# A recurrent pass with two-step triangular solves, products read straight from PSUM, and another order of steps on four engines

## The chip, the cores and the metric

The kernel runs on one core of one Trainium2 chip. The metric is the device time of one launch in microseconds (us): 3440.19 us, the median of three runs (3438.79 to 3451.68). TensorE multiplies matrices into PSUM (8 banks of 128 x 512 numbers), VectorE and ScalarE read PSUM and SBUF, GpSimd reads SBUF and issues the gathers, SyncE issues the other transfers. Each engine works through its own list in order and waits on semaphores where the code says `wait_ge`.

## What is computed

A layer norm, then two branches whose sum is added to the input. The attention branch is a gated delta rule over 16 sequences' halves of 128 tokens, for 16 key heads and 32 value heads of 128 columns; the other branch picks, for each token and each of 8 heads, 8 of 2048 experts, and mixes their rows.

```
mixed = silu(causal conv of width 4 over [q, k, v]);  q, k: l2norm
step: state = state * exp(g_t);  delta = (v_t - state·k_t) * beta_t
      state = state + k_t ⊗ delta;  o_t = state·q_t
y = rmsnorm(o * silu(z)) * norm_w;  attention = y @ w_out
z_e = silu((h · down_embed[e]) * softmax(score));  ffn = sum_e z_e * up_embed[e]
out = x + attention + ffn
```

The recurrence is done in chunks of 128 tokens. For each chunk the kernel solves a unit lower triangular system of 128 x 128, whose off-diagonal part is k·kᵀ times decay and beta.

## The kernel before

After a routing stage, which picks the experts and ends near 290 us, the kernel works through 64 passes (`PASSES`), written out one after another. A pass is one key head of one group of four token tiles; with two value heads (`R`) it has eight tasks, `task(b, c, r)`: b is one of two sequences, c the first or second chunk of it, r the value head. Passes are pipelined in two stages. The front of pass n+1 (projections, convolution, products, the inverses of the 16 x 16 diagonal blocks) is interleaved with the back of pass n (the rest of the inverse, the recurrence over c = 0 and 1, the output). Buffers with a 2 in their name alternate.

**Front.** TensorE: `differences` sums gates (ScalarE makes the decays `DT` with Exp), `projection(u)` for u = 0 (key), 1 (query), 2, 3 (values), 4, 5 (z). ScalarE takes a projection into `raw` and `qkv` (`take`), VectorE adds three `tap`s, ScalarE does `silu` and squares. `products(0)` is k·kᵀ; VectorE's `strict_part` masks it into `km`, and `triangle` makes the eight matrices `AT`. SyncE writes `AT` to DRAM and reads the diagonal blocks back to `bk`; VectorE inverts all of them at once (`eliminate`, `lower_products`, `lower_sums`, `lower_scaled`, `lower_block`, then a copy to `xrT`, `elim_v`); SyncE writes them out and reads them back as `X16` and `XT16` (`inv_in`). `products(1)` is k·qᵀ; `causal_part` masks it into `kq`, and GpSimd multiplies it by `DT` into `MT`.

**Back.** The inverse grows from blocks of 16 to 128 in three levels. Level `lv` is `level_E` on TensorE, a masking multiplication by VectorE (`level`, L1165), and `level_X`, which multiplies on the left and, except in the last level, also makes the other orientation; ScalarE takes both back (`take_X`, `take_XT`). Then for c = 0: `y0_t` = inverse · right side, VectorE scales it (`scaled_y`, L1287), the state `S` and the output; the same for c = 1 after VectorE has corrected the right side `RV` (L1362). `gated` makes `xg`, ScalarE sums its squares, VectorE makes `rms`, GpSimd's `finish` raises it to the power -0.5 and scales the eight tiles of `xg`, TensorE transposes them (`finish_transposes`, L491) and multiplies by `wo` (`finish_out`), VectorE adds to `acc` (`add_outputs`).

**Experts.** In each pass GpSimd gathers 16 rows (L952), in two runs of 8: the first after VectorE's level 1, the second after `mix_v`, the end of the mixing. Between them stands `finish`. VectorE does 16 `expert_dot`s at the pass's start and 16 steps of `expert_mix`.

GpSimd ends its pass with the power for the norms (`norm_p`, L980) and the two multiplications for `MT` (`mt_p`, L984). VectorE waits for `norm_p` after the dots. In VectorE's list `gated(0)`, which waits for `o0_t` from TensorE, stands between `lower_sums` and `lower_scaled`:

```
                if back:
                    dve.wait_ge(sm["yt_t"], at("yt_t", 2))
                    dve.wait_ge(sm["o0_t"], at("o0_t", 1))
                    gated(0, ps[:, 4, :], rq_b, z_b)
                if front:
                    lower_scaled()
```

## Time and profile before

| | us |
|---|---|
| median of three runs | 3440.19 |
| the profiled execution | 3440.67 |
| its span, first to last instruction | 3438.8 |
| TensorE busy | 2992.4 (87%) |
| VectorE busy | 3012.3 (88%) |
| ScalarE busy | 1794.2 (52%) |
| GpSimd busy | 2306.0 (67%) |

The span runs from the first to the last instruction of the program on the core; busy time counts an engine's own instructions, not its waits or its issuing of transfers. A busy share is a mean over routing, passes and tail, so what a step is worth is read in one pass. In a timeline each row is a run of like instructions: start, length, engine, line, what is written and read, how many, and in brackets how long the engine was idle before and what ended it.

### The profile page before, as it was taken

Reading aid. Unit: us, or ns where it says so; the run is one execution under the profiler, and the core shown is the slowest. Engines: PE = TensorE matmul, PEld = TensorE weight load, DVE = VectorE, ACT = ScalarE, POOL = GpSimd, SP = SyncE. Lnnn points to the kernel's source line nnn. Section 1 sums busy time; section 2 is a strip of 40 time slices with the busy share of each in tenths; the row PEclk is TensorE's granted clock in tenths of the full one; section 3 lists DMA queues with packets and bytes.
Section 4 is the critical chain, followed back from the end, with each engine's and each line's share of the span. In section 5 each row is a group of like instructions: output and inputs, shape, how many; then the busy total and the mean of one; then the engine's idle time right before and its main releaser. Section 6 shows DMA issues by size and latency. Waiting matters only on the chain.

```text
span 3438.8 us, 56504 instructions
## 1 busy us (share of the span) xinstructions
PE 2992.4 (87%) x18444; PEld 2451.1 (71%) x18444; DVE 3012.3 (88%) x9101; ACT 1794.2 (52%) x4111; POOL 2306.0 (67%) x2650
## 2 busy tenths in 40 slices
PE   7844999989998989899989988898989899998997
PEld 4422777778776777677767777777777777777776
DVE  5996999989998999899989898998899898989996
ACT  3322555555554555455545555555555555555553
POOL 0005777777767776777778777877777667877764
PEclk9976999999999999999999999999999999999999
DMA  1003545544555545454545554544555454544553
GB/s 60 1 1 104 137 132 141 135 131 132 137 139 135 131 133 139 130 133 133 141 126 138 134 138 124 149 127 134 138 138 137 125 139 132 146 129 135 144 132 89
DMA packets 541827, 427.98 MB, mean 124 GB/s; under 512 B 247008, under 2 KB 450784, under 8 KB 541536
## 3 DMA queue, kind: packets, MB, share of 16 engines
...
q14 instruction: 142, 1.16, 0.1%
...
## 4 chain that ended last, share of the span: by engine, by line
DVE 36%; POOL 35%; PE 14%; issue 9%; DMA 5%; ACT 1%; SPq 0%; DVEq 0%; POOLq 0%; ACTq 0%
POOL rows L952 22%; DVE rows L1193 9%; POOL xg L931 9%; DVE qkv L1177 6%; DVE mix L1210 4%; POOL rms L928 3%; DVE E L1165 3%; DMA rows<-table,pick 3%; PE ps L579 3%; PE ps L500 3%; PE ps L517 2%; PE ps L665 1%; DVE topi L1024 1%; DVE xg L1147 1%; PE ps L521 1%
## 5 line engine op out<-in xcount | busy, mean ns | idle before, releaser
L952 POOL DMA_INDIRECT rows<-table,pick x1024 | 1157.2, 1130 | 326.3 <-issue 326.3
L551 PE MATMUL ps<-X,AT 128*128 128x128 f32 x3072 | 417.7, 294 | 119.2 <-DMA XT<-whole 119.2
L551 PEld LDWEIGHTS ps<-X,AT 128*128 128x128 f32 x3072 | 392.9, 207 | 169.8 <-DMA XT<-whole 167.3
L806 ACT ACTIVATE qkv<-qkv 128x512 f32<-128x512 f32 x256 | 161.5, 631 | 518.6 <-DVE qkv L1177 518.6
L571 PE MATMUL ps<-XT,E 128*128 128x128 f32 x3072 | 400.6, 277 | 0.0
L801 ACT ACTIVATE raw<-ps 128x512 f32<-128x512 f32 x256 | 152.8, 597 | 433.2 <-PE ps L517 433.2
L1210 DVE SCALAR_TENSOR_TENSOR mix<-rows,zc,mix 128x256 f32<-128x256 f32 x896 | 375.1, 476 | 0.0
L571 PEld LDWEIGHTS ps<-XT,E 128*128 128x128 f32 x3072 | 368.9, 192 | 0.0
L939 POOL TENSOR_SCALAR gm<-cst,gn 128x128 f32<-128x128 f32 x512 | 362.9, 723 | 6.7
L1193 DVE CUSTOM_DVE_ANT_0 rows<-rows,h2c 128x128 f32<-128x128 f32 x1024 | 342.9, 399 | 9.2 <-SPq L328 4.7
L931 POOL TENSOR_SCALAR xg<-xg,rms 128x128 f32<-128x128 f32 x520 | 324.9, 637 | 7.0
L564 PEld LDWEIGHTS ps<-E,XT 128*128 128x128 f32 x2048 | 257.7, 193 | 98.1 <-DVE E L1165 56.5
L1177 DVE SCALAR_TENSOR_TENSOR qkv<-raw,cwv,qkv 128x510 f32<-128x510 f32 (+2 forms) x384 | 307.7, 802 | 6.8
L1177 DVE SCALAR_TENSOR_TENSOR qkv<-raw,cwkq,qkv 128x510 f32<-128x510 f32 (+2 forms) x384 | 285.7, 744 | 21.4 <-ACT qkv L802 12.1
L564 PE MATMUL ps<-E,XT 128*128 128x128 f32 x2048 | 274.1, 277 | 26.4 <-DVE E L1165 26.4
L943 POOL COPY pick<-idx_all 128x16 uint32<-128x16 uint32 x64 | 12.6, 196 | 421.9 <-DVE E L1165 421.9
L816 ACT ACTIVATE XT<-ps 128x512 f32<-128x512 f32 x384 | 228.0, 594 | 94.3 <-PE ps L571 86.4
L517 PE MATMUL ps<-xnT,Wkq 128*128 128x512 f32 x512 | 273.6, 661 | 0.0
L1165 DVE TENSOR_TENSOR E<-ps,cst 128x512 f32<-128x512 f32 x384 | 253.2, 682 | 14.6 <-PE ps L551 9.1
L517 PE MATMUL ps<-xnT,Wvz 128*128 128x512 f32 x512 | 254.2, 622 | 0.0
L500 PE MATMUL ps<-wo,yT 128*128 128x256 f32 x1040 | 247.6, 382 | 0.0
L521 PE MATMUL ps<-Wvz,xb 128*128 128x256 f32 x1024 | 243.1, 381 | 0.0
...
## 6 DMA issues: line engine op xcount, KB each, us to landing
...
whole<-AT SPq DMA_DIRECT2D x128, 256.0 KB, 3.6
X<-whole SPq DMA_DIRECT2D x128, 256.0 KB, 3.9
XT<-whole SPq DMA_DIRECT2D x128, 256.0 KB, 4.4
...
```

The costliest lines, as they stand in the source:

```text
L500: done = mm(ps[:, 2 + g, c * D:(c + 1) * D], yT[:, task(g, c, r), :], wo[:, r, :], start=r == 0, stop=r == R - 1)
L517: done = mm(ps[:, bank, :], w[:, k, :], xnT[:, k, bass.ds(pn * N, N)], start=k == 0, stop=k == KD - 1)
L551: done = mm(ps[:, g, (a % 4) * P:(a % 4 + 1) * P], AT_b[:, a, :], src[:, a, :], start=True, stop=True)
L564: done = mm(ps[:, 2 + g, (a % 4) * P:(a % 4 + 1) * P], src[:, a, :], E[:, a, :], start=True, stop=True)
L571: done = mm(ps[:, 4 + g, (a % 4) * P:(a % 4 + 1) * P], E[:, a, :], src[:, a, :], start=True, stop=True)
L931: pool.tensor_scalar(xg[:, a, :], xg[:, a, :], rms[:, a:a + 1], None, ALU.mult).then_inc(sm["y_p"], 1)
L939: pool.tensor_scalar(gm[:, a, :], mask(C_LE), gn[:, a:a + 1], None, ALU.mult).then_inc(sm["gm_p"], 1)
L952: pool.indirect_dma_start(rows[:, m, :], None, table[:, :], bass.IndirectOffsetOnAxis(ap=pick[:, m:m + 1], axis=0)).then_inc(gathered, 16)
L1165: V.tensor_tensor(E[:, 4 * g:4 * g + 4, :], ps[:, g, :].rearrange("p (a i) -> p a i", a=4), mask(C_MS + lv, 4), ALU.mult)\
L1177: ins = V.scalar_tensor_tensor(out=o, in0=i, scalar=w, in1=o, op0=ALU.mult, op1=ALU.add)
L1193: st.did(V.tensor_tensor_reduce(out=rows[:, k, 0:P], in0=rows[:, k, 0:P], in1=h2c[:, :], scale=1.0, scalar=0.0, op0=ALU.mult, op1=ALU.add, ...
L1210: sums[s] = st.did(V.scalar_tensor_tensor(out=mix[:, s, :], in0=rows[:, m, P:ROW], scalar=zc[:, 1, m:m + 1], in1=mix[:, s, :], op0=ALU.mul ...
```

## The change

- **Two steps, then halves.** The levels for 32 and 64 remain (`level_E`, `level_X` with lv 0 and 1), and `level_X` makes one orientation. In the first, VectorE copies the off-diagonal blocks into `E0`, whose diagonal is set once, with a predicated copy; then it turns the result with its own transpose (`turn_X`) for the other orientation. In the second, ScalarE copies two blocks of 32 x 32 per task into `E1` (`take_E`). The last level is gone. Each chunk's solve is now four steps: `blocks` (both halves' own inverses), `carried` (the lower half's correction from the upper 64 rows), `lower_rhs` on VectorE, `blocks` again.
- **Products from PSUM.** `km` and `kq` are gone. GpSimd makes the decays causal (`causal`, an affine select over 128 x 512), ScalarE multiplies them by beta and the key norm (`scale_decays`), and VectorE multiplies them with the products in PSUM: two instructions for `AT`, two for `MT`. Beta goes into the decays; the sign is in `AT`, and its diagonal is no longer set.
- **GpSimd.** `gm` is made by two affine selects, not eight multiplications; `finish` comes first, then both runs of gathers (the first waits for `half_v`, VectorE's mixing of the first four experts); the copies `pick` and `h2c` and the `MT` multiplications are gone.
- **VectorE.** The dots come in two runs of eight; the order is new, with `gated(0)` behind the elimination.
- `xb` and its transfer are gone; TensorE reads `xnT`.

```diff
-LEVELS = [16, 32, 64]
...
+    off = (p // (2 * BL) == j // (2 * BL)) & (p // BL == j // BL + 1)
...
-        E = sb("E", [P, TASKS, P])
-        Y = E
+        E0 = sb("E0", [P, TASKS, P])
+        E1 = sb("E1", [P, TASKS, P])
+        Y = sb("Y", [P, 2, 4, P])
...
-                def level_E(lv):
...
+                def level_E(lv, g):
...
                 def level_X(lv, g):
...
-                    if lv < len(LEVELS) - 1:
-                        for a in range(4 * g, 4 * g + 4):
-                            done = mm(ps[:, 2 + g, (a % 4) * P:(a % 4 + 1) * P], src[:, a, :], E[:, a, :], start=True, stop=True)
-                        done.then_inc(sm["x_t"], 1)
...
+                    E, src = (E1, XT) if lv else (E0, XT16)
                     for a in range(4 * g, 4 * g + 4):
                         done = mm(ps[:, 4 + g, (a % 4) * P:(a % 4 + 1) * P], E[:, a, :], src[:, a, :], start=True, stop=True)
                     done.then_inc(sm["xt_t"], 1)
...
+                def blocks(c, bank):
+                    return four(bank, c, lambda b, r, a: XT[:, a, :], lambda i, a: RV[:, a, :])
+
+                def carried(c, bank):
+                    return four(bank, c, lambda b, r, a: AT_b[0:64, a, :], lambda i, a: Y[0:64, c, i, :])
...
+                    pe.wait_ge(sm["exp_done"], at("exp_done", 2))
+                    products(0)
+                    pe.wait_ge(sm["tap_s"], at("tap_s", 2))
+                    squares(0, 7)
...
+                        pe.wait_ge(sm["e_v"], at("e_v", g + 1))
...
+                        level_X(0, g)
+                    for g in range(2):
+                        pe.wait_ge(sm["x_v"], at("x_v", g + 1))
+                        level_E(1, g)
...
+                        pe.wait_ge(sm["xt_s"], at("xt_s", g + 1))
+                        pe.wait_ge(sm["e_s"], at("e_s", 2 * g + 2))
+                        level_X(1, g)
...
+                    blocks(0, 1).then_inc(sm["y0_t"], 1)
...
+                    pe.wait_ge(sm["top0_s"], at("top0_s", 1))
+                    carried(0, 0).then_inc(sm["u0_t"], 1)
...
+                    pe.wait_ge(sm["at_v"], at("at_v", 2))
+                    products(1)
+                    squares(1, 5)
...
+                    pe.wait_ge(sm["u0_v"], at("u0_v", 1))
+                    blocks(0, 1).then_inc(sm["w0_t"], 1)
...
+                    pe.wait_ge(sm["ys0_s"], at("ys0_s", 1))
...
+                    blocks(1, 0).then_inc(sm["y1_t"], 1)
...
+                    pe.wait_ge(sm["top1_s"], at("top1_s", 1))
+                    carried(1, 1).then_inc(sm["u1_t"], 1)
+                    finish_out(0)
+                    pe.wait_ge(sm["u1_v"], at("u1_v", 1))
+                    blocks(1, 0).then_inc(sm["w1_t"], 1)
+                    finish_out(1)
+                    pe.wait_ge(sm["ys1_s"], at("ys1_s", 1))
+                    four(4, 1, lambda b, r, a: MT_b[:, a, :], lambda i, a: Y[:, 1, i, :]).then_inc(sm["o1_t"], 1)
...
+                def take_E(g):
+
+                    act.wait_ge(sm["e_t"], at("e_t", 3 + g))
+                    for p in (32, 96):
+                        A(E1[p:p + 32, 4 * g:4 * g + 4, p - 32:p], ps[p:p + 32, g, :].rearrange("p (a i) -> p a i", a=4)[:, :, p - 32:p],
+                          ACT.Copy).then_inc(sm["e_s"], 1)
...
+                    if lv == 0:
+                        act.wait_ge(sm["x_v"], at("x_v", g + 1))
...
+                def scale_decays(r):
+
+                    for a in range(r, TASKS, R):
+                        A(DT[:, a, :], DT[:, a, :], ACT.Copy, scale=scol[:, a:a + 1]).then_inc(sm["scaled_s"], 1)
+
+                def take_Y(c, rows, bank):
+                    return A(Y[0:rows, c, :, :], ps[0:rows, bank, :].rearrange("p (i d) -> p i d", i=4), ACT.Copy)
...
+                    act.wait_ge(sm["s_v"], at("s_v", 1))
+                    act.wait_ge(sm["causal_p"], at("causal_p", 2))
+                    scale_decays(0)
...
+                    scale_decays(1)
...
+            def causal(dst, src, done):
+
+                pool.affine_select(dst, src, [[0, 4], [1, P]], ALU.is_ge, zero, base=0, channel_multiplier=-1).then_inc(done, 1)
...
-                for a in range(TASKS):
-                    pool.tensor_scalar(gm[:, a, :], mask(C_LE), gn[:, a:a + 1], None, ALU.mult).then_inc(sm["gm_p"], 1)
...
+                for g in range(2):
+                    causal(gm[:, 4 * g:4 * g + 4, :], gn[:, 4 * g:4 * g + 4].unsqueeze(2).broadcast_to([P, 4, P]), sm["gm_p"])
...
+                for g in range(2):
+                    pool.wait_ge(sm["exp_done"], at("exp_done", g + 1))
+                    d = DT[:, 4 * g:4 * g + 4, :]
+                    causal(d, d, sm["causal_p"])
...
-                    pool.wait_ge(sm["e_v"], at("e_v", 3))
-                picks(f)
-                pool.tensor_copy(h2c[:, :], h2_all[:, bass.ds(f // 4, 1), :].rearrange("p a c -> p (a c)"))
-                gather(0)
+                    finish()
+                    pool.wait_ge(sm["half_v"], at("half_v", 1))
+                gather(f, 0)
                 if n is not None:
-                    finish()
                     pool.wait_ge(sm["mix_v"], at("mix_v", 1))
-                gather(K // 2)
+                gather(f, K // 2)
...
-                for g in range(2):
-                    pool.tensor_tensor(MT2[nx][:, 4 * g:4 * g + 4, :].rearrange("p (t r) i -> p t r i", r=R),
...
+                    V.copy_predicated(E0[:, 4 * g:4 * g + 4, :], mask(C_OFF, 4).bitcast(U32), ps[:, g, :].rearrange("p (a i) -> p a i", a=4))\
...
+                    V.transpose(X[:, 4 * g:4 * g + 4, :].rearrange("p a i -> p (a i)"), ps[:, 4 + g, :]).then_inc(sm["x_v"], 1)
...
-                    for a in range(4 * g, 4 * g + 4):
-                        st.did(V.scalar_tensor_tensor(out=AT[:, a, :], in0=km[:, a // R, :], scalar=scol[:, a:a + 1], in1=DT[:, a, :],
-                                                      op0=ALU.mult, op1=ALU.mult))
-                    st.wait()
-                    V.tensor_tensor(AT[:, 4 * g:4 * g + 4, :], AT[:, 4 * g:4 * g + 4, :], mask(C_ID, 4), ALU.add).then_inc(sm["at_v"], 1)
...
+                def triangle(r):
+
+                    dve.wait_ge(sm["scaled_s"], at("scaled_s", 4 * r + 4))
+                    V.scalar_tensor_tensor(out=of_head(AT, r), in0=keys_by_time(), scalar=-1.0, in1=of_head(DT, r), op0=ALU.mult, op1=ALU.mult)\
+                        .then_inc(sm["at_v"], 1)
...
+                def lower_rhs(c, bank, ready, done):
+
+                    dve.wait_ge(sm[ready], at(ready, 1))
+                    v = half_tasks(RV, c)[64:P].rearrange("p b r d -> p b (r d)")
+                    V.tensor_tensor(v, ps[64:P, bank, :].rearrange("p (b d) -> p b d", b=2), v, ALU.add).then_inc(sm[done], 1)
...
+                    for r in range(R):
+                        V.tensor_tensor(of_head(MT, r), keys_by_time(), of_head(DT, r), ALU.mult).then_inc(sm["mt_v"], 1)
...
                         dve.wait_ge(sm["norm_p"], last("norm_p"))
+                    second_outputs()
+                    second_gated(nx)
+                    dve.wait_ge(gathered[0], 128 * n + 128)
+                    expert_dots(0, (0, 1))
+                    expert_weights(0)
...
+                    key_norms()
+                if back:
+                    turn_X(0)
+                    turn_X(1)
...
+                    expert_mix(6, 8)
+
+                    st.wait()
+                    V.tensor_tensor(total, mix[:, 0, :], mix[:, 1, :], ALU.add).then_inc(sm["mix_v"], 1)
+                if front:
+                    lower_products()
+                    lower_sums()
+                    lower_scaled()
+                    lower_block()
+                    st.wait()
+                    V.tensor_copy(xrT[:, :, :], rows_of(xr).rearrange("n i c -> n c i")).then_inc(sm["elim_v"], 1)
+                if back:
+                    dve.wait_ge(sm["yt_t"], at("yt_t", 2))
+                    dve.wait_ge(sm["o0_t"], at("o0_t", 1))
+                    gated(0, ps[:, 4, :], rq_b, z_b)
+                    lower_rhs(1, 1, "u1_t", "u1_v")
+                if front:
+                    for u in (2, 3):
+                        for d in (1, 2, 3):
+                            tap(u, d)
```

On **TensorE**, before, from the last level's end to the second chunk's output (L571 level_X, L517 and L521 projections, L579 solves, state and outputs, L491 transposes, L500 output, L665 state products):

```order
L571 MATMUL ps<-XT,E 128x128 x8
L517 MATMUL ps<-xnT,Wvz 128x512 x2
L579 MATMUL ps<-RV,XT 128x128 x4
L491 MATMUL ps<-cst,xg 128x128 x8
L517 MATMUL ps<-xnT,Wvz 128x512 x2
L579 MATMUL ps<-E,Kd 128x128 x4
L579 MATMUL ps<-E,MT 128x128 x4
L500 MATMUL ps<-wo,yT 128x256 x4
L521 MATMUL ps<-Wvz,xb 128x256 x4
L665 MATMUL ps<-S,qkv 128x256 x4
```

Now, from the same place to the state products (L562 is every solve, L533 and L540 the products and squares of the front):

```order
L554 MATMUL ps<-XT,E 128x128 x8
L625 MATMUL ps<-cst,qkv 128x128 x2
L516 MATMUL ps<-xnT,Wvz 128x512 x2
L562 MATMUL ps<-RV,XT 128x128 x4
L490 MATMUL ps<-cst,xg 128x128 x8
L562 MATMUL ps<-Y,AT 128x128 x4
L533 MATMUL ps<-qkv 128x128 x4
L540 MATMUL ps<-ones,sq 128x1 x4
L562 MATMUL ps<-RV,XT 128x128 x4
L516 MATMUL ps<-xnT,Wvz 128x512 x2
L562 MATMUL ps<-Y,Kd 128x128 x4
L562 MATMUL ps<-Y,MT 128x128 x4
```

The solve of the first chunk has two groups more, and steps of the front stand between its steps.

On **VectorE**, before, the end of the elimination and of the pass:

```order
L1232 TENSOR_TENSOR prod<-bk,xr 64x512
L1240 TENSOR_REDUCE low<-prod 64x64
L1147 SCALAR_TENSOR_TENSOR xg<-ps,norm,z 128x256 x2
L1246 TENSOR_TENSOR prod<-xr,low 64x512
L1255 TENSOR_REDUCE xr<-prod 64x8x8
L1354 COPY xrT<-xr 64x256
```

Now, from the correction of `RV` (L1405) and the last mixing (L1260, L1410) on:

```order
L1405 SCALAR_TENSOR_TENSOR RV<-ps,neg,RV 128x128 x4
L1260 SCALAR_TENSOR_TENSOR mix<-rows,zc,mix 128x256 x4
L1410 TENSOR_TENSOR acc<-mix 128x256
L1285 TENSOR_TENSOR prod<-bk,xr 64x512
L1293 TENSOR_REDUCE low<-prod 64x64
L1299 TENSOR_TENSOR prod<-xr,low 64x512
L1308 TENSOR_REDUCE xr<-prod 64x8x8
L1417 COPY xrT<-xr 64x256
L1185 SCALAR_TENSOR_TENSOR xg<-ps,norm,z 128x256 x2
L1328 TENSOR_TENSOR RV<-ps,RV 64x2x256
```

`gated` (L1147, now L1185) has moved behind the elimination, and the mixing's end, which stood ahead of the elimination, into the middle of it.

On **GpSimd**, one pass before:

```order
L964 COPY cols<-gates 128x24
L966 COPY xr<-cst 64x256
L935 COPY gn<-gates 128x8
L939 TENSOR_SCALAR gm<-cst,gn 128x128 x8
L943 COPY pick<-idx_all 128x16
L973 COPY h2c<-h_all 128x128
L952 DMA rows<-table,pick 128x384 x8
L928 TENSOR_TENSOR rms<-rms,powers 128x8
L931 TENSOR_SCALAR xg<-xg,rms 128x128 x8
L952 DMA rows<-table,pick 128x384 x8
L980 TENSOR_TENSOR norm<-ss,powers 128x8
L984 TENSOR_TENSOR MT<-kq,DT 128x512 x2
```

and now:

```order
L1004 COPY cols<-gates 128x24
L1006 COPY xr<-cst 64x256
L977 AFFINE_SELECT DT<-DT 128x512 x2
L981 COPY gn<-gates 128x8
L977 AFFINE_SELECT gm<-gn 128x512 x2
L968 TENSOR_TENSOR rms<-rms,powers 128x8
L971 TENSOR_SCALAR xg<-xg,rms 128x128 x8
L992 DMA rows<-table,idx_all 128x384 x16
L1021 TENSOR_TENSOR norm<-ss,powers 128x8
```

The power and the scaling of `xg` stand ahead of all 16 gathers.

## Rows read from the trace of the kernel before

**Rows 1.** The page, part 1: busy time, share of the span, instructions of each engine.

```profile
PE 2992.4 (87%) x18444; PEld 2451.1 (71%) x18444; DVE 3012.3 (88%) x9101; ACT 1794.2 (52%) x4111; POOL 2306.0 (67%) x2650
```

**Rows 2.** Timeline of SyncE's queue: pass starts (L346), AT out (L353), last pass (L335).

```profile
1794.30 0.35 SPq L346 DMA_DIRECT2D Wvz<-wvz  x1
...
1809.47 2.23 SPq L353 DMA_DIRECT2D whole<-AT  x2
...
1841.89 0.34 SPq L346 DMA_DIRECT2D Wvz<-wvz  x1
...
3387.45 29.35 SPq L335 DMA_DIRECT2D wo<-woh  x2
```

**Rows 3.** Stretches: us, busy of PE, PEld, DVE, ACT, POOL; granted clock; DMA.

```profile
1794.30:1799.70 5.40, 5.37 (x21) 3.86 (x22) 5.30 (x27) 1.30 (x2) 4.56 (x7) 0.68 0.77 241
...
333.30:3388.20 3054.90, 2760.60 (x17517) 2308.23 (x17518) 2731.77 (x7591) 1682.59 (x3906) 2250.87 (x2574) 0.97 0.51 135
```

**Rows 4.** Timeline of TensorE, from one pass into the next.

```profile
1823.73 0.66 PE L491 MATMUL ps<-cst,xg 128*128 128x128 f32 x4 [1.66 <-POOL xg L931]
...
1841.92 2.70 PE L551 MATMUL ps<-X,AT 128*128 128x128 f32 x16 [1.88 <-DMA XT<-whole]
...
1850.77 1.95 PE L551 MATMUL ps<-X,AT 128*128 128x128 f32 x16
...
1857.12 1.06 PE L571 MATMUL ps<-XT,E 128*128 128x128 f32 x8
1858.01 1.06 PE L564 MATMUL ps<-E,XT 128*128 128x128 f32 x8
```

**Rows 5.** Timeline of VectorE, from one pass into the next.

```profile
1819.77 0.23 DVE L1222 TENSOR_TENSOR outer<-bk,xr 64x14 f32<-64x14 f32 x1 [0.55 <-DMA bk<-whole]
...
1821.89 0.74 DVE L1287 TENSOR_TENSOR E<-ps,scol 128x256 f32<-128x256 f32 x2
...
1828.00 0.88 DVE L1147 SCALAR_TENSOR_TENSOR xg<-ps,norm,z 128x256 f32<-128x256 f32 x2 [2.14 <-PE ps L579]
...
1830.61 0.37 DVE L1354 COPY xrT<-xr 64x256 f32<-64x256 f32 x1
...
1838.35 2.17 DVE L1193 CUSTOM_DVE_ANT_0 rows<-rows,h2c 128x128 f32<-128x128 f32 x1
...
1840.67 0.28 DVE L1193 CUSTOM_DVE_ANT_0 rows<-rows,h2c 128x128 f32<-128x128 f32 x1
...
1849.38 2.30 DVE L1177 SCALAR_TENSOR_TENSOR qkv<-raw,cwkq,qkv 128x510 f32<-128x510 f32 x3
...
1852.39 1.28 DVE L1165 TENSOR_TENSOR E<-ps,cst 128x512 f32<-128x512 f32 x2
...
1862.39 1.66 DVE L1210 SCALAR_TENSOR_TENSOR mix<-rows,zc,mix 128x256 f32<-128x256 f32 x4
```

**Rows 6.** Timeline of GpSimd, one pass, and one row of another pass.

```profile
1027.77 1.19 POOL L952 DMA_INDIRECT rows<-table,pick  x1 [5.07 <-issue]
...
1823.86 1.08 POOL L952 DMA_INDIRECT rows<-table,pick  x1 [0.18 <-issue]
...
1834.32 1.39 POOL L952 DMA_INDIRECT rows<-table,pick  x1 [0.30 <-issue]
1835.72 1.69 POOL L980 TENSOR_TENSOR norm<-ss,powers 128x8 f32<-128x8 f32 x1
1837.39 2.49 POOL L984 TENSOR_TENSOR MT<-kq,DT 128x512 f32<-128x512 f32 x2
...
1840.67 5.74 POOL L939 TENSOR_SCALAR gm<-cst,gn 128x128 f32<-128x128 f32 x8
...
1866.29 4.94 POOL L931 TENSOR_SCALAR xg<-xg,rms 128x128 f32<-128x128 f32 x8
```

**Rows 7.** Timeline of ScalarE, two rows of one pass.

```profile
1810.67 0.60 ACT L816 ACTIVATE XT<-ps 128x512 f32<-128x512 f32 x1
...
1816.24 1.16 ACT L870 ACTIVATE Kd<-ps,cols 128x128 f32<-128x128 f32 x4
```

422 lines of the change are left out of this document (186 added, 236 removed).

## The prediction

> **What bounds the kernel now.** I read the page first, then stretches, then the four timelines of one pass. The page has TensorE at 87% and VectorE at 88% [rows 1], so no engine is full, and the mean doesn't say what ends last. The passes start at SyncE's loads of `Wvz`, 1794.30 and 1841.89 [rows 2], 47.6 us apart, and all 63 full passes take 3054.9 us [rows 3], 48.5 each. So the question is which ring of waits closes in 47.6 us.
>
> Read backwards from TensorE's L551, which idles 1.88 us for the DMA of `XT` and starts at 1841.92 [rows 4]. That DMA hangs on VectorE's copy to `xrT`, ended at 1830.98 [rows 5]: 10.9 us out to DRAM and back. The copy stands behind `gated`, for which VectorE idled 2.14 us, waiting for TensorE's output of the first chunk [rows 5]. That sits behind TensorE's list from 1794.3 on, in which it waits once more, 1.66 us, for GpSimd's scaled `xg` [rows 4]. The ring is: TensorE's levels, the wait for GpSimd, the first chunk, `gated`, the elimination's end, two DMAs. Also, at the pass's start the granted clock is 0.68 over 5.4 us [rows 3], part of it at 1.2 GHz: 16 products take 2.70 us there and 1.95 later [rows 4]. It fell after TensorE had been idle for 1.88 us. A mean of 0.68 is 3.5 us at half speed, a loss of 1.7; the mean of 0.97 over all passes [rows 3] is 1.45 us lost in each.
>
> **What the change takes off that ring.** `gated` now stands behind the elimination, so the copy to `xrT` no longer waits for TensorE, and `level_E` waits behind `projection(0)`. TensorE loses two groups of four products in each of two `level_X`, one whole `level_E` and one whole `level_X`, eight groups; four are added by `carried` and the second `blocks`. A group is 0.89 us, start to start [rows 4]: 3.6 us less of TensorE's time. VectorE loses two pairs of masks (1.28 each, [rows 5]) for one pair of transposes, the `km` and `kq` products, and most of `triangle`; it gains two `MT` products and pays two `lower_rhs` for two `scaled_y`. It also loses 1.9 us at the first dot, which took 2.17 us against 0.28 for the others [rows 5], and ended 0.6 us after GpSimd's `MT` (1837.39 to 1839.88, [rows 6]). That multiplication has left GpSimd. `xb`, `pick` and `h2c` cost nothing on a ring: SyncE's queue and GpSimd both waited there.
>
> **The ring that takes its place.** Gathers 9 to 16 can't start before `mix_v`, since their rows are being read. GpSimd then does 8 gathers and the power, and VectorE's first instruction of the next pass, the addition to `QS`, now waits for `norm_p`. Before, the gathers started at 1823.86, 4.6 us after the mixing had ended, and VectorE needed the norms only behind 16 dots. I walk this ring once, from `norm_p` at 0:
>
> - `QS`, `gated`, eight dots with their weights, three taps: 0.7 + 0.9 + 2.15 + 2.2 = 5.95. (512 columns from PSUM 0.64, `gated` 0.88, dots 0.24 apart, taps 2.30 for three, [rows 5].) TensorE, freed 3.8 us before `norm_p`, has `projection(0)` done by then and `level_E` too, as `inv_in` comes 10.9 us after an elimination that ends 9.9 us before this point.
> - ScalarE's `silu` 0.7, then `products(0)`, `squares(0)` and two groups of `level_X`: 3.8, to 10.45.
> - The second transpose 0.65 (below), `take_XT` 0.6, eight scalings and two copies: 11.1, 11.85, then 4 x 0.29 + 0.6 + 4 x 0.29 to 14.9. (A copy 0.60, four scaled copies 1.16, [rows 7].) VectorE idles some 2.3 us here, filled only by one expert.
> - `AT` of the second head 0.7: 15.6. Two experts mixed 1.6 ([rows 5]: four steps 1.66), taps 2.4 with a short wait, eight dots 2.1: 21.7. `lower_rhs` 0.65 and `MT` 1.3 with 0.75 of waits for TensorE: 24.4. Two experts: 26.0.
> - The diagonal blocks are back by then: between the second half of `AT` going out (1809.47 to 1811.70, [rows 2]) and the first elimination step (1819.77, [rows 5]) lie 8.1 us, and 15.6 + 8.5 is 24.1. The whole elimination took 1830.98 - 1819.77 - 2.14 - 0.80 - 0.74 = 7.5 us [rows 5]; its first part, 3.6, stands on the ring: 29.6. `RV` 1.1, the last two experts and the sum 2.0: `mix_v` at 32.75.
> - GpSimd: from 1823.86 to 1835.72 eight gathers, 11.86, then the power 1.69, and 0.2 ahead [rows 6]: 13.75. `norm_p` at 46.5.
>
> The other end of the pass is shorter: after `mix_v` VectorE has 3.9 of elimination, `gated`, `lower_rhs`, six taps and the additions, 11.2 us, and TensorE's last product ends some 3.8 us before `norm_p`.
>
> **Prices that the trace doesn't show.** The predicated copy and the transpose: 128 x 512 out of PSUM in one instruction, so I take the mask's 0.64; half of that at best, double at worst. Doubled, the transposes add 1.3 on the ring and the copies 0.6. The Trainium skill's page Vector Engine (DVE) Microarchitecture Reference, section The reshape front-end and per-opcode configuration, states one element per cycle and lane for the transpose; no run here shows it. The affine selects: 1.25, as `MT`'s (two in 2.49) have the shape; from 0.4 to 2.9, the latter four times the 0.72 of a `gm` tile of a quarter the width (eight in 5.74, [rows 6]). GpSimd then reaches `finish` at 7.4, as VectorE's `rms` does, and ends it at 14.2 (1.7 + 0.1 + 5, [rows 6]), where TensorE wants it at 20; even at 2.9 it ends at 19.2. The first gathers wait for VectorE's fourth expert (17.2) and end at 28, before `mix_v`, so the selects are hidden up to 3.2 us each.
>
> **The clock.** TensorE idles 2.8 us ahead of `products(0)`, longer than the 1.88 after which it fell. If it falls, the 1.7 us are lost on the ring, since products, squares and `level_X` follow. Between 0 and 1.7 I take 1.0: 47.5 us a pass.
>
> **Stalls.** One gather in 113 begins after 5.07 us of idling [rows 6], seven times in the trace, always in the first run of eight; most of what lies between 47.6 and the mean of 48.5 us is theirs. Now the first run has 4.7 us to spare, so I take 1 us each, 7 in all.
>
> **Sum.** Routing and the first front 333.3 + 3 for two copies of `E0` and `E1`; 63 x 47.5 = 2992.5; the last pass and the tail as before, 3438.8 - 3387.45 = 51.4 [rows 2, 3]; 7 of stalls; 1.9 around the span: 3389 us. The profiled execution took 3440.67, the median is 3440.19, so they stand alike.
>
> **Rivals.** About 0.5%, 17 us, is what a measurement can tell from no change; that is 0.27 us a pass.
>
> - *A shorter ring.* The clock holds and the eight gathers, 9.8 to 10 us without company (eight of 0.95 and 0.30 between), end sooner, or the transposes cost half: 44.9 to 46.5 us, 3225 to 3326. For it: each select and copy that left GpSimd. Against: the eight gathers' 11.86 had VectorE's taps and elimination beside them, as they will now. From about 45 us on TensorE's last product sets the pass. Chance 0.22.
> - *One for one.* The `norm_p` ring and small waits I set at 0.1 make up what the DMA ring gave: 48.1 to 48.6 us, 3423 to 3457. Chance 0.12.
> - *Slower: VectorE held at the pass's start.* Four affine selects run at GpSimd from 0.5 to 6 us, just beside `gated`, the dots and the taps. If each holds VectorE as `MT` held the first dot, two pairs cost 1.9 each, all on the ring before `products(0)`: 51.3 at worst, 49.4 with one pair, 3509 to 3630. It decides from 1.1 us of holding on. The row of the first dot speaks for it; that the dots beside `gm` took 0.28 [rows 5, 6] speaks against. The Trainium skill's page GPSIMD Engine Reference, section Key points, names contention with VectorE's instructions that have two SBUF inputs, which a dot and a tap are; the trace agrees for `MT`, not for `gm`. Doubled prices of the new VectorE instructions, 49.4, fall in the same place. Chance 0.23.
> - *Slower: selects above 3.2 us each.* Then `finish` delays TensorE's transposes, and each 0.1 us costs 0.4: at 4 us a pass has 50.7. The same page of the Trainium skill, section Elementwise — side-by-side cycle accounting, states about 12 cycles an element for data-dependent branching, by which a select would take 5.1 us, an estimate; no row here shows it. Chance 0.05.
>
> My forecast, 46.5 to 48.1 us, has 0.38. Faster by over 0.5%: 0.38 + 0.22 = 0.60; within: 0.12; slower: 0.28. The range leaves out one in ten on either side: 3230 (the clock holds and the gathers are short) to 3520 (one pair of selects holds VectorE, with a little more).
>
> **What would show it.** Right: L1191 (`QS`) idles for GpSimd's `norm`, and TensorE no longer for `XT`; the gathers of L992 start right behind the last mixing and take near 11.9; VectorE idles between L1213 and L1239 for ScalarE; `finish` ends before TensorE's L490; copy and transpose near 0.68. Wrong: L1191 idles for TensorE, which would put the bound on the solves; dots or taps beside the selects well over 0.28 and 0.77; L490 idles for GpSimd; or passes above 48.1 us with all prices as taken, and then a wait that I missed.

## The result and the profile after

| | before | changed |
|---|---|---|
| median of 4 runs each | 3441.15 us (3438.79 to 3451.68) | 3601.57 us (3586.55 to 3609.83) |
| profiled execution, its span | 3440.67, 3438.8 us | 3607.9, 3606.2 us |
| 63 full passes | 3054.9 us, 48.5 each | 3555.95 - 327.9 = 3228.1 us, 51.2 each |

The ratio is 1.0454, with an interval of 1.0416 to 1.0492: slower, where I had forecast 3389 us and faster. 3601.57 lies above my range too. Ratios and intervals here and below are of fast runs alone, while the medians in us are of all runs, among them one slow run of e2 (4808.36 us), one of e4 (4195.36 us) and some of e5 to e8 and e14.

The page of the changed kernel, part 1, against [rows 1]:

```profile
PE 2997.9 (83%) x16396; PEld 2358.0 (65%) x16396; DVE 2745.4 (76%) x8461; ACT 1944.6 (54%) x4815; POOL 1902.9 (53%) x2140
```

VectorE has 267 us less to do and GpSimd 403. TensorE has 2048 instructions less and yet is busy 5 us longer, which only slower instructions can do. The work that was to go is gone, and every engine idles more than before: the time is in waits and in the clock. The starts of two passes in SyncE's queue, and of the last (against [rows 2]):

```profile
1816.33 0.35 SPq L346 DMA_DIRECT2D Wvz<-wvz  x1
...
1867.59 0.34 SPq L346 DMA_DIRECT2D Wvz<-wvz  x1
...
3555.95 30.57 SPq L335 DMA_DIRECT2D wo<-woh  x2
```

A pass has 51.26 us here. The first of VectorE's waits (engine, line, releaser: us in total, times, longest):

```profile
DVE QS L1191 <- POOL norm L1021: 163.9, 63, 2.9
```

So VectorE's first instruction of each pass waits 2.6 us for GpSimd's power, 63 times of 63. Its timeline from one pass into the next, against [rows 5]:

```profile
1848.62 1.13 DVE L1405 SCALAR_TENSOR_TENSOR RV<-ps,neg,RV 128x128 f32<-128x128 f32 x4 [0.59 <-PE ps L659]
...
1851.36 0.42 DVE L1410 TENSOR_TENSOR acc<-mix 128x256 f32<-128x256 f32 x1
...
1865.67 0.69 DVE L1191 TENSOR_TENSOR QS<-ps,QS 128x512 f32<-128x512 f32 x1 [2.60 <-POOL norm L1021]
1866.40 1.32 DVE L1185 SCALAR_TENSOR_TENSOR xg<-QS,norm,z 128x256 f32<-128x256 f32 x2
...
1867.85 0.76 DVE L1243 CUSTOM_DVE_ANT_0 rows<-rows,h_all 128x128 f32<-128x128 f32 x1
...
1868.54 0.70 DVE L1243 CUSTOM_DVE_ANT_0 rows<-rows,h_all 128x128 f32<-128x128 f32 x1
...
1870.43 2.31 DVE L1224 SCALAR_TENSOR_TENSOR qkv<-raw,cwkq,qkv 128x510 f32<-128x510 f32 x3
1872.65 1.34 DVE L1207 COPY_PREDICATED E<-cst,ps 128x512 f32<-128x512 uint32 x2
...
1879.04 0.72 DVE L1213 STREAM_TRANSPOSE X<-ps 128x512 f32<-128x512 f32 x1 [0.89 <-PE ps L554]
1880.45 0.72 DVE L1213 STREAM_TRANSPOSE X<-ps 128x512 f32<-128x512 f32 x1 [0.69 <-PE ps L554]
```

GpSimd in the same stretch, against [rows 6]: the second eight gathers begin 0.3 us behind the mixing's sum (L1410), then comes the power, then what ran beside `gated` and the dots.

```profile
1852.06 1.51 POOL L992 DMA_INDIRECT rows<-table,idx_all  x1 [5.91 <-DVE acc L1410]
...
1862.88 0.95 POOL L992 DMA_INDIRECT rows<-table,idx_all  x1 [0.30 <-issue]
1863.86 1.68 POOL L1021 TENSOR_TENSOR norm<-ss,powers 128x8 f32<-128x8 f32 x1
...
1866.01 1.42 POOL L977 TENSOR_SCALAR_AFFINE_SELECT DT<-DT 128x512 f32<-128x512 f32 x2
1867.39 0.37 POOL L981 COPY gn<-gates 128x8 f32<-128x8 f32 x1
1867.83 1.27 POOL L977 TENSOR_SCALAR_AFFINE_SELECT gm<-gn 128x512 f32<-128x512 f32 x2
```

TensorE at the pass's start, against [rows 4]. The 16 products of L547 at 1867.62 take 2.05 us; then it idles for ScalarE's `silu`, and the same work takes longer:

```profile
1867.62 2.05 PE L547 MATMUL ps<-X,AT 128*128 128x128 f32 x16 [0.80 <-DMA XT<-whole]
...
1873.54 2.04 PE L533 MATMUL ps<-qkv 128*128 128x128 f32 x8 [3.00 <-ACT qkv L813]
1875.38 1.71 PE L540 MATMUL ps<-ones,sq 128*128 128x1 f32 x8
1876.95 3.47 PE L554 MATMUL ps<-XT,E 128*128 128x128 f32 x16
```

The stretches of that pass (us, busy of PE, PEld, DVE, ACT, POOL; granted clock; DMA share, GB/s), against [rows 3]:

```profile
1865.67:1873.54 7.87, 4.08 (x27) 2.91 (x26) 7.73 (x25) 4.56 (x14) 3.36 (x7) 0.97 0.44 149
1873.54:1884.88 11.34, 11.34 (x60) 10.19 (x60) 4.96 (x15) 5.43 (x16) 6.47 (x9) 0.72 0.03 7
1884.88:1902.98 18.10, 16.94 (x106) 13.88 (x106) 15.54 (x57) 12.46 (x29) 8.41 (x8) 1.00 0.47 132
1902.98:1916.86 13.88, 11.58 (x57) 8.24 (x56) 10.91 (x17) 6.61 (x17) 11.45 (x11) 1.00 0.67 168
```

0.72 over 11.34 us is 6.3 us at 1.2 GHz and the rest at 2.4, all of it behind the wait. In the records the half speed lasts 6.8 us of each pass, in 62 passes of 62, and begins some 0.4 us before the wait ends (7.47 us behind `QS`, where `products(0)` starts at 7.88); in the kernel before it was 2.9 us a pass. The wait is 3.00 us in these rows and 3.3 us in the median of the passes.

Between instants of a pass I compare kernels by their medians over the full passes, counted from the start of `QS` (us). The taps and `mix_v` are taken at their ends, the other steps at their starts; the last column is the mean length of 62 passes, and in the first row it is the walk plus my 1.0 for the clock.

| | end of taps | `products(0)` | 2nd transpose | 2nd half of `AT` | elimination | `mix_v` | pass |
|---|---|---|---|---|---|---|---|
| my walk | 5.95 | 6.65 | 10.45 | 14.9 | 26.0 | 32.75 | 46.5 + 1.0 |
| changed | 7.07 | 7.88 | 14.78 | 19.21 | 30.62 | 37.31 | 51.2 |
| e1 | 7.07 | 7.79 | 11.66 | 16.09 | 27.50 | 34.20 | 48.1 |
| e11 | 5.73 | 6.98 | 10.75 | 15.18 | 26.61 | 33.29 | 47.2 |
| e9 | 7.67 | 8.53 | 12.37 | 16.80 | 28.22 | 34.91 | 46.2 |

### The profile page after: what moved, and what is told of

It is laid out like the page before. It is cut to its first block, busy times and chain, and to the rows that moved or that the text cites. A ratio compares the mean times of both kernels' runs of the same rounds, so it can differ in the third digit from the quotient of the medians.

```text
span 3606.2 us, 51837 instructions
## 1 busy us (share of the span) xinstructions
PE 2997.9 (83%) x16396; PEld 2358.0 (65%) x16396; DVE 2745.4 (76%) x8461; ACT 1944.6 (54%) x4815; POOL 1902.9 (53%) x2140
## 4 chain that ended last, share of the span: by engine, by line
PE 36%; DVE 26%; POOL 18%; ACT 11%; issue 8%; DMA 1%; SPq 0%; DVEq 0%; POOLq 0%; ACTq 0%
POOL rows L992 15%; PE ps L562 9%; PE ps L516 7%; PE ps L554 6%; PE ps L533 5%; DVE rows L1243 4%; ACT DT L839 4%; PE ps L540 4%; DVE qkv L1224 4%; POOL norm L1021 3%; DVE mix L1260 3%; DVE xg L1185 2%; DVE RV L1405 2%; PE ps L659 2%; ACT E L826 2%
## 5 line engine op out<-in xcount | busy, mean ns | idle before, releaser
L992 POOL DMA_INDIRECT rows<-table,idx_all x1024 | 1139.8, 1113 | 1043.6 <-DVEq L1264 427.5
L533 PE MATMUL ps<-qkv 128*128 128x128 f32 x1024 | 203.7, 361 | 205.1 <-ACT qkv L813 205.1
L1260 DVE SCALAR_TENSOR_TENSOR mix<-rows,zc,mix 128x256 f32<-128x256 f32 x896 | 373.5, 475 | 0.0
L533 PEld LDWEIGHTS ps<-qkv 128*128 128x128 f32 x1024 | 174.6, 257 | 227.5 <-issue 219.9
L562 PEld LDWEIGHTS ps<-RV,XT 128*128 128x128 f32 x2048 | 258.6, 191 | 88.7 <-DVE RV L1328 53.8
L547 PEld LDWEIGHTS ps<-X,AT 128*128 128x128 f32 x2048 | 245.4, 193 | 101.3 <-DMA XT<-whole 94.0
L562 PE MATMUL ps<-RV,XT 128*128 128x128 f32 x2048 | 282.0, 281 | 29.2 <-DVE RV L1328 28.3
L547 PE MATMUL ps<-X,AT 128*128 128x128 f32 x2048 | 269.3, 283 | 42.4 <-DMA XT<-whole 42.4
L968 POOL TENSOR_TENSOR rms<-rms,powers 128x8 f32<-128x8 f32 x65 | 116.8, 1796 | 346.0 <-DVE rms L1173 346.0
L1243 DVE CUSTOM_DVE_ANT_0 rows<-rows,h_all 128x128 f32<-128x128 f32 x1024 | 283.0, 338 | 0.2 <-DVE mix L1260 0.2
L520 PE MATMUL ps<-Wvz,xnT 128*128 128x256 f32 x1024 | 241.9, 379 | 0.0
```

The costliest lines, as they stand in the source:

```text
L520: done = mm(ps[:, bank, (t % 2) * 256:(t % 2) * 256 + 256], xnT[:, k, pn * N + t * P:pn * N + (t + 1) * P], Wvz[:, k, 2 * P:4 * P], start= ...
L533: done = mm(ps[:, 6, t * P:(t + 1) * P], qkv[:, KCH, t * P:(t + 1) * P], qkv[:, w, t * P:(t + 1) * P], start=True, stop=True)
L547: done = mm(ps[:, g, (a % 4) * P:(a % 4 + 1) * P], AT_b[:, a, :], src[:, a, :], start=True, stop=True)
L562: done = mm(ps[:, bank, i * P:(i + 1) * P], lhs(b, r, task(b, c, r)), rhs(i, task(b, c, r)), start=True, stop=True)
L992: pool.indirect_dma_start(rows[:, m, :], None, table[:, :], bass.IndirectOffsetOnAxis(ap=idx_all[:, f // 4, (f % 4) * 16 + m:(f % 4) * 16 ...
L1243: st.did(V.tensor_tensor_reduce(out=rows[:, k, 0:P], in0=rows[:, k, 0:P], in1=h2_all[:, n // 4, :], scale=1.0, scalar=0.0, op0=ALU.mult, o ...
```

## The experiments

Theory A: the clock falls behind TensorE's wait before `products(0)`, and the ring pays for it. Theory D: GpSimd's selects hold VectorE at the pass's start. Both presuppose the ring through the second gathers and the power.

**e1.** In the changed kernel, three products that nobody reads, into a free bank, in TensorE's wait:

```
                     pe.wait_ge(sm["exp_done"], at("exp_done", 2))
+                    for _ in range(3 if back else 0):
+                        mm(ps[:, 6, :], mask(C_ID), xnT[:, 0, 0:N], start=True, stop=True)
                     products(0)
```

> The changed kernel, with three extra 128x512 products (they read a mask and xnT, write PSUM bank 6, and products(0) overwrites them) in TensorE's list right ahead of products(0), where it idles 3.06 us in every pass. The rest is untouched. Theory A (clock): the granted clock falls because of this idle stretch, and the stretch from products(0) to the end of the second level_E, 8.7 us in the changed kernel, runs at half speed on the ring that sets the pass; kept busy, TensorE stays at full speed, the stretch takes 5.4 us and a pass 51.3 - 3.3 = 48.0 us, 3400 us in all. Theory B (the ring is GpSimd's gathers and norm, and TensorE's speed is hidden behind ScalarE's scalings): no change beyond 0.3 us a pass, 3580 to 3620 us. Theory C (TensorE is the bound): 2.6 us more a pass, 3770 us.

Measured: 3417.38 us, 0.9919 of before (0.9891 to 0.9947). The clock was at half speed in none of the 62 passes between the first and the last. TensorE's timeline of e1, where L603 are the three products:

```profile
1832.42 1.04 PE L597 MATMUL ps<-cst,qkv 128*128 128x128 f32 x8
1833.30 2.74 PE L603 MATMUL ps<-xnT,cst 128*128 128x512 f32 x6
1835.91 1.16 PE L533 MATMUL ps<-qkv 128*128 128x128 f32 x8
1836.90 0.95 PE L540 MATMUL ps<-ones,sq 128*128 128x1 f32 x8
1837.72 2.03 PE L554 MATMUL ps<-XT,E 128*128 128x128 f32 x16
```

With 2.7 us of added work the pass is 3.1 us shorter, and all of it between `products(0)` and the second transpose (3.87 us where it was 6.90). Theory A holds, with three times my price. (Beside e1 to e4 the kernel before took 3445.32 us.)

**e2.** The power and its wait moved ahead of the second eight gathers:

```
                 gather(f, 0)
+                pool.wait_ge(sm["ssk_v"], at("ssk_v", 2))
+                pool.tensor_tensor(norm2[nx]..., both, ALU.pow).then_inc(sm["norm_p"], 1)
                 if n is not None:
                     pool.wait_ge(sm["mix_v"], at("mix_v", 1))
                 gather(f, K // 2)
-                pool.wait_ge(sm["ssk_v"], at("ssk_v", 2))
-                pool.tensor_tensor(norm2[nx]..., both, ALU.pow).then_inc(sm["norm_p"], 1)
```

> The changed kernel, with GpSimd's power for norm_p moved from behind the second run of gathers to between the two runs, where GpSimd idles 5.9 us. Theory B (the ring closes over mix_v, eight gathers, power, norm_p, QS): VectorE no longer waits 2.6 us for norm_p, QS follows the additions, and a pass loses 2.4 to 2.8 us: 3430 to 3455 us; and if with it TensorE's idle stretch ahead of products(0) shrinks to under 1.5 us, as ScalarE's take of the projection is then what VectorE waits for, the clock drop goes too (theory A), another 2 to 3.3 us: down to 3230 us. Rival (TensorE's solves are the bound, and QS would wait for them as long): 0 to 1 us, 3540 to 3600 us.

Measured: 3308.68 us, 0.9591 (0.9561 to 0.9621), 137 us less than the kernel before beside it (3445.32) and 293 less than the changed kernel. `QS` no longer waits, the pass has 46.3 us, and the wait of L533 falls from 205.1 us to this:

```profile
PE ps L533 <- ACT qkv L813: 66.9, 62, 4.4
```

The records have 7 falls of the clock in 62 passes, where the changed kernel has 62. One edit took away the ring and most of the clock's loss.

**e3.** GpSimd waits for the weights of the first dots (`dot_v`) before the copies and the selects.

```
+                if n is not None:
+                    pool.wait_ge(sm["dot_v"], at("dot_v", 1))
                 pool.tensor_copy(cols2[nx][:, :, :]...
```

> The changed kernel, with GpSimd's copies and affine selects held until VectorE's first eight dots are done (a wait for dot_v). Theory D (contention): gated takes 0.9 instead of 1.3 us and the dots 2.0 instead of 2.7, so silu and products(0) come 1.1 us earlier: a pass of 50.2 us, 3535 us. Theory A alone: nothing that the contention gives can be kept while the clock drop stays, or more is lost or won as the drop moves: 51.3 or, without it, 47 us. If the selects now hold the taps: 51.3 us or more.

Measured: 3598.97 us, 1.0458 (1.0429 to 1.0488): nothing gained. The dots did shrink (all at 0.29), but the taps did not stay. VectorE in e3:

```profile
1807.61 3.65 DVE L1226 SCALAR_TENSOR_TENSOR qkv<-raw,cwkq,qkv 128x510 f32<-128x510 f32 x3
```

3.65 us where they took 2.31. The selects cost VectorE the same 1.3 us, now beside the taps, and their end stays at 7.07 us behind `QS`. D as I had put it (dots alone) fell; as "the selects hold whatever VectorE does beside them" it was still open.

**e4.** e2 and e3 together.

> Both of the last two edits. If they are separate costs on one ring: the sum, about 3.7 us a pass off 51.3, 3370 us, and less if the clock drop goes. If QS then waits for TensorE's last product: no better than the early norm alone.

Measured: 3337.4 us, 0.9671 (0.9633 to 0.9709), worse than e2 alone; the clock falls 23 times in place of 7, though the wait before `products(0)` is 1.3 us in the median, little more than the 1.1 of e2.

**e5 to e8** were run on another chip, and can't be compared with e1 to e4: beside them the kernel before took 3476.61 us (3454.64 to 3517.01), and their traces have waits that no instruction of the core ends ("remote"), none of which is in the traces of before, after and e1 to e4. Their kernels ran again as e9 to e12, on a chip without them. e5 is the kernel before with two idle products ahead of its L551 (first diff); e6 is e1 and e2 together; e7 is e1 with the selects of `DT` behind the third tap and those of `gm` behind `finish` (second diff); e8 is e2 with the same.

```
                 if place["u"]:
-                    pe.wait_ge(sm["inv_in"], last("inv_in"))
                     pe.wait_ge(sm["ys1_v"], last("ys1_v"))
+                for _ in range(2 if back else 0):
+                    mm(ps[:, 0, :], mask(C_ID), xnT[:, 0, 0:N], start=True, stop=True)
+                if place["u"]:
+                    pe.wait_ge(sm["inv_in"], last("inv_in"))
                 if back:
                     level_E(0)
```

```
+                if n is not None:
+                    pool.wait_ge(sm["conv_v"], at("conv_v", 1))
                 for g in range(2):
                     pool.wait_ge(sm["exp_done"], at("exp_done", g + 1))
                     d = DT[:, 4 * g:4 * g + 4, :]
                     causal(d, d, sm["causal_p"])
+                if n is not None:
+                    finish()
                 if f + 1 < PASSES:
                     gate_sums(f + 1, 2 if n is None else 1)
                 if n is not None:
-                    finish()
                     pool.wait_ge(sm["half_v"], at("half_v", 1))
```

> The kernel before, with two products of 128x512 whose result nobody reads, ahead of TensorE's wait for the DMA XT<-whole, in the 1.85 us in which it idles there. In the trace of before the clock is at half speed 2.9 us per pass right behind that gap (L551 2.88 us where 1.95 at full speed, L517 2.76 where 1.98): 1.7 us. If those stand on before's ring, as I read it, 63 passes give back some 105 us: about 3340 us, ratio 0.97. If before's ring goes past them (the drop is paid from slack), it stays within 0.5% of 3445 us. Either way the changed kernel's loss to the clock is then seen against a kernel before without one.

> The changed kernel with the power moved ahead of the second eight gathers (as e2) and three idle products ahead of products(0) (as e1). Theory VectorE-bound: in e2 no wait for GpSimd is left at QS and the 46.3 us of a pass are VectorE's own instructions and its short waits for the other engines; the clock fell in 7 of 62 passes only, 0.44 us of half speed per pass, of which half is lost time: 14 us at the most, so 3295 to 3309 us. Theory clock still a term of its own: below 3290 us.

> e1 (clock held, ring through the gathers intact) with GpSimd's two selects of DT behind VectorE's third tap and the two selects of gm behind the root mean square's work, in GpSimd's idle time. Theory contention: in e1 the stretch from QS to the end of the three taps takes 7.07 us where 5.95 were predicted from rows without a neighbour; in e3 the selects waited for the dots and the dots shrank by 1.3 us, but the taps grew from 2.31 to 3.65 us. So the selects cost VectorE 1.1 us wherever they run beside its first-chunk work, and behind the taps they cost nothing on the ring: the pass falls from 48.1 to 47.0 us, 3417 less 69: about 3350 us. Rival (the loss comes from elsewhere, or the selects then stretch the copies E by as much): within 0.5% of 3417 us.

> e2 (power ahead of the second gathers) with the selects put behind the taps and behind the root mean square's work. In e2 gated, dots and taps take 7.68 us from QS, 1.7 more than the 5.95 of rows without a neighbour. Theory contention on VectorE's ring: a pass of 46.3 falls by 1.5, 3309 less 95: about 3215 us. Rival: the 1.7 us move to the idle time before products(0) and the clock drops there again, as in the changed kernel: 3290 us or more.

Measured there: e5 1.0001 (0.9921 to 1.0082), e6 1.0574 (1.0485 to 1.0664), e7 1.0518 (1.0427 to 1.0609), e8 1.0371 (1.0283 to 1.0459). Nothing follows from them on the theories.

**e9 to e12.** e2's kernel, e8's, e7's and e5's again.

> The kernel of e2, again, as the measure for the next three: beside e5 to e8 the kernel before itself took 3477 us with a spread of 60 us, and in e8's trace ScalarE and VectorE show waits of up to 5 us that no instruction of this core ends (57 times before L842), so those four can't be set against e1 to e4. If that was a disturbance of that chip at that time, e2's kernel stands at 0.959 of before again; if the timing of these kernels differs from chip to chip, it doesn't.

> The kernel of e8 again, beside e2's. Theory contention on VectorE's ring: 1.5 us of a pass less than e9, 0.97 of e9's time, ratio to before 0.932. Rival: the freed time becomes idle time of TensorE before products(0) and a clock drop there, ratio 0.955 or more.

> The kernel of e7 again: e1 with the selects behind the taps. Theory contention: 1.1 us of a pass less than e1 (ratio 0.9919), so 0.972. In e7's disturbed trace gated, dots and taps did shrink to 5.73 us (7.07 in e1), but products(0) came at 7.18 only (7.79 in e1), since ScalarE's squares and the activation of the weights end later than the taps: then only 0.6 to 0.9 us come off the pass, 0.975 to 0.981. Rival: nothing, 0.992.

> The kernel of e5 again. In e5 the two extra products ahead of L551 gave 1.000 with an interval of 0.8% either way. If the clock drops of before stand on its ring, 0.97; if they are paid from slack, or the drop moves elsewhere, 1.00.

| | us | ratio to before (3441.88) | interval |
|---|---|---|---|
| e9 | 3312.59 | 0.9640 | 0.9624 to 0.9656 |
| e10 | 3315.69 | 0.9635 | 0.9617 to 0.9653 |
| e11 | 3372.23 | 0.9809 | 0.9793 to 0.9825 |
| e12 | 3437.92 | 0.9992 | 0.9977 to 1.0006 |

e11 against e1 (0.9919) shows theory D on the ring: with the selects behind the taps, the taps end at 5.73 in place of 7.07 and the pass has 47.2 us in place of 48.1. VectorE still waits for GpSimd, and `gated` is back at 0.88:

```profile
1801.44 0.69 DVE L1196 TENSOR_TENSOR QS<-ps,QS 128x512 f32<-128x512 f32 x1 [2.60 <-POOL norm L1026]
1802.17 0.88 DVE L1190 SCALAR_TENSOR_TENSOR xg<-QS,norm,z 128x256 f32<-128x256 f32 x2
...
1804.78 0.17 DVE L1353 TENSOR_TENSOR zc<-dot,prob_all 128x8 f32<-128x8 f32 x1
1804.86 2.31 DVE L1229 SCALAR_TENSOR_TENSOR qkv<-raw,cwkq,qkv 128x510 f32<-128x510 f32 x3
1807.09 1.35 DVE L1212 COPY_PREDICATED E<-cst,ps 128x512 f32<-128x512 uint32 x2
```

GpSimd's selects of `DT` now run beside the two copies into `E0`, which read one input from SBUF and one from PSUM: 1.35 us, where they took 1.34 without them. Of the 1.34 us 0.9 came through: `silu` begins 1.3 us earlier, but the three idle products of e1 now end after it (1805.86 + 2.74 = 1808.60 in e11's trace), and `products(0)` waits for them. e10 shows the same edit worth nothing once the ring is broken. There the dots end earlier and the taps wait for ScalarE's copy of `projection(0)`:

```profile
1828.81 0.68 DVE L1194 TENSOR_TENSOR QS<-ps,QS 128x512 f32<-128x512 f32 x1
...
1834.02 2.32 DVE L1227 SCALAR_TENSOR_TENSOR qkv<-raw,cwkq,qkv 128x510 f32<-128x510 f32 x3 [1.51 <-ACT qkv L809]
```

e12 contradicts my reading of the kernel before. The two idle products cut L551's wait from 119.2 us in all to

```profile
PE ps L551 <- DMA XT<-whole: 23.9, 41, 1.7
```

and the mean clock of the passes rose from 0.97 to 0.99 (9 falls in 62 passes, 44 before), and no time came off. Counted from L551's start, medians of 63 passes, level 1's products come at 8.26 us where before had 8.81, but VectorE's mask of level 1 at 10.29 against 10.38 and `gated` at 33.47 against 33.62: what TensorE gained it waited for VectorE. So the work behind L551 had slack, and neither the clock nor, as far as L551 waits for it, the DMA of `XT` set before's pass. What stayed the same is VectorE's wait for `gated`, 197.5 and 198.6 us, and ahead of it TensorE's wait for GpSimd's scaled `xg` (L491), 137.6 and 140.1 us. Which work ahead of that wait sets its end wasn't tried; what the profile's chain says of it stands below.

**e13 to e15** ran on another chip, with the late signals of e5 to e8 again (the waits called "remote"). e13 is e6's kernel; e14 and e15 are e1 with `range(1 if back else 0)` and `range(2 if back else 0)`: one and two idle products in place of three.

> The kernel of e6 again (power ahead of the second gathers, three idle products ahead of products(0)), since e6 fell into a disturbance. e9 is the same without the idle products: 0.964 of before, clock at half speed 0.33 us per pass. TensorE's wait before products(0) there is 0.98 us of a pass and three products need 2.7: they end later than the activation they fill the wait for, so products(0) come later. Theory ring on TensorE and VectorE: 0.97 to 0.985, slower than e9. Theory clock still a term: 0.960.

> As e1, with one idle product in place of three: the wait of 3.0 us before products(0) is cut to about 2.1. If the length of the gap decides whether the clock falls, and 2.1 us is still enough, the time is that of the changed kernel, 1.045 of before; if one product keeps it, 0.992 as e1. Nothing in the traces says where between them it changes; in before the clock fell behind gaps of 1.85 us.

> As e1, with two idle products: a wait of about 1.2 us is left before products(0). In e2, with 0.98 us per pass left there, the clock fell in 7 of 62 passes only. So I expect nearly e1's time: 0.992 to 1.000 of before.

**e16 to e18**, the changed kernel itself, e14's and e6's again, met yet another chip with late signals.

> The changed kernel itself, unedited, as the measure for the two beside it. Where the chip shows none of the late signals of e5 to e8 and e13 to e15 (waits of 3 to 5 us of VectorE or ScalarE for a TensorE instruction long ended), 1.045 of before as in the result, by every theory; where it shows them, 1.10 or more, as e14 and e15 then did with most of the clock's loss removed.

> The kernel of e14 again: one idle product ahead of products(0). In e14's trace, on a chip with late signals, the stretch from products(0) to the end of the second level took 5.4 us (median), between the 6.9 of the changed kernel and the 3.8 of e1 with three: so the clock falls in a part of the passes. The time then lies between: 1.00 to 1.035 of before. Were the whole gap of 3 us needed for the fall, it would be e1's 0.992.

> The kernel of e6 and e13 again. Against e9 (0.964): theory ring on TensorE and VectorE, with products(0) later by the 1.2 us that e6 and e13 showed (9.8 us behind QS where e9 has 8.5): 47.4 us per pass, 0.985. Theory clock still a term: 0.960.

Measured: e13 1.0981 (1.0939 to 1.1023), e14 1.1320 (1.1257 to 1.1383), e15 1.1075 (1.1031 to 1.1118), with before at 3485.51 us; e16 1.1286 (1.1225 to 1.1348), e17 1.1007 (1.0953 to 1.1062), e18 1.0685 (1.0638 to 1.0733), with before at 3496.46. The late signals lie in the middle of the pass. VectorE and TensorE in e15, around `carried` and what waits for it:

```profile
1842.81 1.16 PE L562 MATMUL ps<-Y,AT 64*128 64x128 f32 x8
1843.90 1.16 PE L533 MATMUL ps<-qkv 128*128 128x128 f32 x8
...
1847.68 0.69 DVE L1330 TENSOR_TENSOR RV<-ps,RV 64x512 f32<-64x512 f32 x1 [4.29 <-remote]
...
1848.43 2.08 PE L562 MATMUL ps<-RV,XT 128*128 128x128 f32 x8 [2.59 <-DVE RV L1330]
1850.54 1.29 DVE L1336 TENSOR_TENSOR MT<-ps,DT 128x512 f32<-128x512 f32 x2 [2.17 <-remote]
```

The products that `RV` needs end at 1843.97 and VectorE starts 3.7 us later; in the changed kernel's own trace that is 0.03 us (1892.31 to 1892.34). The times of these six runs therefore say nothing on A and D. But the stretch from `products(0)` to the end of the second level lies ahead of the disturbance and takes 3.8 us at full speed and 6.9 at half, so it still counts how often the clock fell there, in 62 passes of each:

| idle products | median wait left before `products(0)` | passes at full speed (under 4.2 us) |
|---|---|---|
| 0 (changed kernel; e16) | 3.3; 3.2 us | 0; 5 |
| 1 (e14; e17) | 2.3; 2.2 us | 29; 32 |
| 2 (e15) | 1.3 us | 60 |
| 3 (e1) | 0.5 us | 62 |

The gap need not be closed: with 1.3 us of waiting left the clock nearly always holds here. But the length of this one wait doesn't decide it across kernels: e4, with the same 1.3 us left, fell in 21 of 62 passes. In e18 the clock held in that stretch in all 62 passes, but `products(0)` came 9.73 us behind `QS`, 1.2 later than in e9; what three products are worth on top of e2 stays open, as no undisturbed run has both.

## Why the prediction was wrong

**The ring: right.** `QS` waits for `norm` in 63 passes of 63, and moving the power alone (e2) took 4.9 us off each pass: by the medians of e9, the same kernel, 2.6 between `mix_v` and `QS` and 3.1 behind `products(0)`, less 0.6 by which the pass's start grew. From `mix_v` to `QS` my term was 13.75, and it is 13.9 (37.31 to 51.2), with eight gathers at 11.8. This is the wait that I named as taking the place of the one removed. What I did not do is compare it with the ring before, which already had eight gathers on it (next point).

**What bounds the kernel before: wrong.** "The ring is: TensorE's levels, the wait for GpSimd, the first chunk, `gated`, the elimination's end, two DMAs" fell with e12: a faster TensorE behind L551 changed nothing. The page of before had another ring, in part 4, the chain of work that ended last (share of the span by engine, then by line):

```profile
DVE 36%; POOL 35%; PE 14%; issue 9%; DMA 5%; ACT 1%; SPq 0%; DVEq 0%; POOLq 0%; ACTq 0%
POOL rows L952 22%; DVE rows L1193 9%; POOL xg L931 9%; DVE qkv L1177 6%; DVE mix L1210 4%; POOL rms L928 3%; DVE E L1165 3%; DMA rows<-table,pick 3%; PE ps L579 3%; PE ps L500 3%; PE ps L517 2%; PE ps L665 1%; DVE topi L1024 1%; DVE xg L1147 1%; PE ps L521 1%
```

VectorE's dots, first taps and the mask of level 1 (L1165) let GpSimd's first eight gathers go; behind them stand the power and the scaling of `xg`, and only then TensorE's transposes, the first chunk and the outputs, and VectorE again. The gathers' 22% are 11.8 us a pass, an estimate from 3438.8 us and 64 passes; the DMA of `XT` is not among these lines. So in the kernel before, too, short results that TensorE needed (`finish`) stood behind eight gathers. The change took them from there and put `norm_p` behind the other eight. This is the profile's reading; no run moved before's gathers. My ring before didn't enter the sum, which walks the new one, but it made a gain seem natural.

**The clock: the term that failed first.** "Between 0 and 1.7 I take 1.0", and the upper bound came from the kernel before, behind a wait of 1.88 us. The wait here is 3.0 us in the rows, the half speed lasts 6.8 us in place of 2.9, and it lies under work on the ring: 3.1 us a pass (51.2 less e1's 48.1). I had seen that the gap is longer, and still priced it by the drop of the kernel before, and by a part of that. The mechanism was right and the term mis-sized: 2.1 us a pass, 132 us in all.

**The pass's start: the second.** I gave `QS`, `gated`, dots and taps 5.95 us from rows without a neighbour; they take 7.07. The two `gated` took 1.32 and two dots 0.76 and 0.70 beside the selects. The mechanism stood among the rivals ("VectorE held at the pass's start", deciding from 1.1 us on) with 0.23, and in the forecast at nothing. It holds VectorE by 1.3 us and costs the pass 0.9 (e1 to e11). The Trainium skill's page GPSIMD Engine Reference, section Key points, whose rule I weighed against the quiet dots beside `gm`, was right here: VectorE's instructions with two SBUF inputs are held beside affine selects of 128 x 512, and e3 shows the taps held as the dots were. The dots beside before's `gm` weren't all quiet either: a quarter of them (228 of 863) took 0.36 or 0.37 in place of 0.28.

**Prices of the new instructions: right or near.** Copy and transpose 0.67 and 0.72 where I took 0.64; an affine select 0.64 (median of 256) where I took 1.25 (0.4 to 2.9), so the select above 3.2 us is refuted; the elimination's first part 2.9 where I had 3.6, given back by the wait for `ks_t` behind it. From the second transpose to `AT` my 4.45 is 4.43, from elimination to `mix_v` 6.75 is 6.69.

**The sum.** My walk to `mix_v` is 32.75 and the trace has 37.31: 1.2 at the start, 3.1 of clock, 0.3 between `AT` and the elimination. Less the 1.0 that I had for the clock, a pass is 3.7 us longer than 47.5: 236 us. The first front ended 8 us earlier than I had it, the stalls of gathers that I priced at 7 us did not come at all, and the last pass is 1 us shorter: 3389 + 236 - 8 - 7 - 1 = 3609, against 3607.9 of the profiled execution.

**The rivals.** A shorter ring and one for one are refuted, and selects above 3.2 us too. The slower case came true in direction by two mechanisms of which I had let each stand alone. With the clock at its full loss of 1.7 and the selects at 1.3 even my own numbers gave 49.5 us, slower than before; the chances should have counted that sum, not each part. That 3601.57 falls into the 3509 to 3630 of "VectorE held at the pass's start" is luck: of the 3.7 us by which a pass exceeds 47.5, at most 1.2 arose there. Two of my signs of being wrong did come, dots well over 0.28 and passes above 48.1.
